# Ten staging tiles for layer 1's table, the plan read ahead of the fourth store, and a clear cut into four

## The reference, cut to what matters

```python
def _cgconv(x, src, dst, edge_attr, Wf, bf, Ws, bs, gamma, beta, rmean, rvar):
    z = jnp.concatenate([x[dst], x[src], edge_attr], axis=-1)      # 128 + 128 + 64
    msg = jax.nn.sigmoid(z @ Wf + bf) * jax.nn.softplus(z @ Ws + bs)
    summed = jax.ops.segment_sum(msg, dst, num_segments=n)
    cnt = jax.ops.segment_sum(jnp.ones((dst.shape[0],), x.dtype), dst, num_segments=n)
    out = summed / jnp.maximum(cnt, 1.0)[:, None]
    out = (out - rmean) * jax.lax.rsqrt(rvar + BN_EPS) * gamma + beta
    return out + x
...
x = _layernorm(x + cgconv(cgconv(x, layer 1), layer 2), axis=-1)
```

## Time and profile before

| | us |
|---|---|
| median of 3 runs | 2125.92 (2125.62 to 2128.58) |
| the profiled execution, its own time | 2123.97 |
| its span, first to last instruction | 2122.2 |

### The profile page before, as it was taken

The page is one execution under the profiler, slowest core; times in us unless marked ns, Lnnn a source line. Parts: engine busy times, 40 slices in busy tenths (PEclk is TensorE's granted clock), DMA queues, the critical chain, the costliest instruction groups (busy, mean ns, idle before and its releaser), DMA issues. The chain is left out here.

```text
span 2122.2 us, 35684 instructions
## 1 busy us (share of the span) xinstructions
PE 1561.2 (74%) x8321; PEld 1286.5 (61%) x8321; DVE 1801.6 (85%) x4351; ACT 1677.1 (79%) x2908; POOL 1513.2 (71%) x1589
## 2 busy tenths in 40 slices
PE   6877776777777777777487777777777777777773
PEld 5666665666566666666466666566665655666662
DVE  4799998989989889898648999899888887988887
ACT  3799887878878878787457888788878887887884
POOL 5577777777777777777257777777777777777770
PEclk8999999989999999999799999899999998998995
DMA  8355555555555555555375555555555555555542
GB/s 277 114 161 166 156 166 155 165 154 156 166 155 155 164 154 155 155 165 154 129 235 154 162 163 158 155 163 165 154 154 156 165 154 154 160 158 155 155 142 62
DMA packets 161806, 336.71 MB, mean 159 GB/s; under 512 B 58866, under 2 KB 85610, under 8 KB 161671
## 3 DMA queue, kind: packets, MB, share of 16 engines
q0 software_dynamic: 74496, 202.13, 32.1%
q1 hardware_dynamic: 85654, 131.58, 20.0%
q10 hardware_dynamic: 1522, 1.72, 0.3%
HBM read 315.49 MB, written 19.81 MB: 158 GB/s over the span
## 5 line engine op out<-in xcount | busy, mean ns | idle before, releaser
L343 POOL DMA_INDIRECT pre<-s_rows,ends x1512 | 1449.7, 959 | 488.7 <-issue 446.0
L457 PE MATMUL pre_ps<-rhs,lhs 128*128 128x256 f32 x3136 | 856.3, 418 | 462.7 <-DVE lhs L696 461.2
L457 PEld LDWEIGHTS pre_ps<-rhs,lhs 128*128 128x128 f32 x3136 | 608.4, 204 | 677.5 <-DVE lhs L696 390.0
L716 DVE TENSOR_TENSOR pre<-pre_ps,pre 128x1024 f32<-128x1024 f32 x378 | 460.4, 1218 | 50.7 <-DMA pre<-s_rows,ends 50.0
L546 ACT ACTIVATE pre<-pre 128x512 f32<-128x512 f32 x392 | 246.9, 630 | 307.7 <-DVE pre L716 268.9
L470 PEld LDWEIGHTS sum_ps<-hot,msg 128*128 128x128 f32 x3136 | 438.7, 203 | 51.8 <-issue 14.4
L696 DVE TENSOR_SCALAR lhs<-lhs,base_f,part 64x256 f32<-64x256 int32 x784 | 342.1, 436 | 114.8 <-issue 107.3
L470 PE MATMUL sum_ps<-hot,msg 128*128 128x64 f32 x3136 | 415.9, 278 | 23.8 <-DVE sums L736 23.8
L551 ACT ACTIVATE logs<-pre 128x1024 f32<-128x1024 f32 x392 | 414.4, 1057 | 12.4
L541 ACT COPY rhs<-dst_ps 64x256 f32<-64x256 f32 x792 | 290.0, 366 | 28.9 <-PE dst_ps L444 12.1
L727 DVE TENSOR_TENSOR msg<-soft_ps,logs 128x512 f32<-128x512 f32 x392 | 270.8, 691 | 13.6
(11 more groups left out here) (88 smaller groups left out, 570.1 us busy)
## 6 DMA issues: line engine op xcount, KB each, us to landing
lhs<-dge_and_destination_cols SPq DMA_DIRECT2D x196, 512.0 KB
pre<-s_rows,ends POOLq DMA_INDIRECT x1512
s_rows<-logs SPq DMA_DIRECT2D x10, 512.0 KB, 8.1
s_rows<-msg SPq DMA_DIRECT2D x7, 512.0 KB, 7.1
x_rows<-pre SPq DMA_DIRECT2D x12, 256.0 KB, 4.5
out<-y_out SPq DMA_DIRECT2D x12, 256.0 KB, 2.3
s_rows<-x_t SPq DMA_DIRECT2D x4, 512.0 KB, 11.9
ends<-edge_ends SPq DMA_DIRECT2D x100, 16.0 KB
```

Of the source, the lines that this page charges most:

```text
L343: nc.gpsimd.indirect_dma_start(pre[:, slot(k, j), i, 0:width], None, rows, bass.IndirectOffsetOnAxis(ap=ends[:, k, j * TILES + i, 0:1], ax ...
L457: ins = nc.tensor.matmul(pre_ps[:, j % 2, i, :], lhs[:, j // 2, edges], rhs[:, j, i // 2, :], start=True, stop=not plain(b, k, j))
L716: nc.vector.tensor_tensor(rows, pre_ps[:, j % 2], rows, ALU.add).then_inc(s_pre[j], 1)
```

## The change

Layer 1's table gets ten staging tiles in place of seven: the first three are in the part of `x1_t` that the sorted-destination test used (so ACT waits for `flagged` before it copies), then `logs`, `hot` and `msg`, then two more parts of `x1_t`. Only stores 10, 11 and 12 use a tile again (0, 1 and 2). `read_plan` now stands behind store 2. ACT's writes to `x1_t` begin three steps later (steps 3 to 27), and wait for the last stores out of tiles 0 to 2 and, at step 15, for tiles 8 and 9. DVE's clear of the counts is cut into four pieces of 1,600 columns, one at the end of each of steps 0 to 3, ahead of `one_hot`; step 4 waits for them.

```diff
         if first:
-            s_stage = [t["x1_t"][:, r * 4 * F2:(r + 1) * 4 * F2].rearrange("p (w f) -> p w f", f=F2) for r in (3, 4)] + s_stage
+            in_x1 = [t["x1_t"][:, r * 4 * F2:(r + 1) * 4 * F2].rearrange("p (w f) -> p w f", f=F2) for r in range(5)]
+            s_stage = in_x1[0:3] + s_stage[0:2] + s_stage[4:5] + s_stage[2:4] + in_x1[3:5]
...
-        log_stages, msg_stages, hot_stage = ((2, 3), (4, 5), 6) if first else ((0, 1), (2, 3), 4)
+        log_stages, msg_stages, hot_stage = ((3, 4), (6, 7), 5) if first else ((0, 1), (2, 3), 4)
...
             if first:
-                for c in range(5):
+                for c in range(3):
                     store_s(c)
                 bodies, at = read_plan()
-                for c in range(5, STORES):
+                for c in range(3, STORES):
                     store_s(c)
...
             if first:
+                act.wait_ge(flagged, 1)
                 for i in range(DOUBLES):
                     stage_double(i)
...
-                    step = SLOTS * k + j
-                    if first and isinstance(b, int) and step == 12:
-                        for r in (0, 1):
+                    step = SLOTS * k + j - 3
+                    if first and isinstance(b, int) and step in (0, 12):
+                        for r in ((0, 1, 2) if step == 0 else (8, 9)):
                             act.wait_ge(s_out[r], stores_of(r))
-                    if first and isinstance(b, int) and step < DOUBLES:
+                    if first and isinstance(b, int) and 0 <= step < DOUBLES:
...
             if first:
-                nc.vector.memset(t["sums"][:, 1, :], 0.0).then_inc(zeroed, 1)
                 v.wait_ge(iotas, 3)
-                v.wait_ge(zeroed, 2)
...
+                if first and isinstance(b, int) and SLOTS * k + j == 4:
+                    v.wait_ge(zeroed, 5)
...
+                if first and isinstance(b, int) and step < 4:
+                    nc.vector.memset(t["sums"][:, 1, step * (NPAD // 4):(step + 1) * (NPAD // 4)], 0.0).then_inc(zeroed, 1)
```

## The result

| | before | changed |
|---|---|---|
| median of 6 runs each | 2125.77 us (2123.27 to 2128.58) | 2115.65 us (2112.61 to 2118.41) |
| the profiled execution | 2123.97 us | 2112.61 us |
| its span | 2122.2 us | 2110.8 us |
| mean granted clock | 0.924 | 0.925 |

The ratio is 0.9954, with a 95% interval of 0.9942 to 0.9965: 10.1 us sooner by the medians. The forecast was 2116.3, in a range of 2112.5 to 2121.5. The changed kernel's profiled execution is the fastest of its six, so between the two traces there are 11.4 us to account for and not 10.

The account below looks back on a forecast made before the run. POOL's gather stream was taken as the bound, so only an earlier start counts: 8.6 + 0.5 + 1.6 - 1.1 = 9.6 us off the 2125.92 us median gives 2116.3 us, range 2112.5 to 2121.5.

Parts of the forecast that it names:

- The bound and the carry: POOL's gather stream, continuous from step 12, sets the pace; time saved ahead of step 5's softplus shortens the whole run equally.
- Part 1: Table's end: with ten stages ACT's last copy waits for PE, not a store, ending at 32.3 for 40.9; gain 8.6 us.
- Part 2: SP's queue: `read_plan` behind store 2 sends base loads near 21.4, and later stores still land in time; gain or loss zero.
- Part 3: Last table copy to step 2's turned rows: the same 15.9 us as before, so step 2 at 48.2.
- the first rival: Start of the steps: clock stays at 2.4 GHz through step 0, saving about 2.2 us; 2114.6 us, chance 0.12.
- Part 4: ACT's `x1_t` writes three steps later: 0.5 us less PE wait for `rhs`, and 1.6 us because the clock holds.
- Part 5: DVE's clear in four pieces, steps 0 to 3: three hidden, the fourth delays step 4; loss 1.1 us.
- The sum: Step 5's softplus 9.6 us sooner, carried by POOL to the end: median 2116.3 us.

Follow-up runs that it names:

- The held PE: The changed kernel with PE made to wait, behind the table, for the store out of a `msg` stage: 2130.21 us, ratio 1.0011.
- the late plan: The changed kernel with `read_plan` back behind the fifth store, the pieces of the clear kept: 2117.25 us, ratio 0.9958.
- the clear in two: The changed kernel with three quarters of the clear ahead of the steps and the last quarter in step 0: 2117.81 us, ratio 0.9957.
- The later writes alone: The kernel before, with only ACT's writes to `x1_t` moved three steps later: 2123.58 us, ratio 0.9987.
- clear on POOL: The changed kernel with POOL clearing the counts in one instruction after its last `x_rows` gather, none on DVE: 2120.48 us, ratio 0.9981.
- the stages alone: The changed kernel with `read_plan` back behind the fifth store and the clear one instruction ahead of the steps: 2113.49 us, ratio 0.9946.

## Why the prediction was right, point by point

**The bound and the carry: right.** POOL's stream ran on from step 12 without a wait, and step 12's 10.95 us are in the span as 11.4 (0.45 more, within the spread of such stretches). The held PE turned this into a test: 12.27 us at step 12, and a ratio of 1.0011.

**Part 1, 8.6 us: right, with 9.3 measured** (40.9 to 31.57). PE finished the table half a microsecond sooner, at 30.95 instead of 31.41; that end isn't the change's doing and lies between 30.35 and 32.56 in the eight traces, so the term is good to about 1 us. The wait for `flagged` was taken as free, and is, though not without a trace: ACT's first table load stood ahead of that wait and now stands behind it, and the first copy begins at 10.23 us instead of 9.03:

```profile
8.93 1.28 ACT L516 ACT_TABLE_LOAD   x1 [8.93 <-PE pre_ps L395]
```

By 11.68 ACT was back at PE's heels, and nothing of it is seen at the table's end.

**Part 2, zero: right.** The base loads went out at 20.65 (forecast 21.4), `hot` was late by 0.81 us (forecast under 1), and the late plan costs 0.5 us at step 0. The hole in the DMA engines' work was expected at 26 to 29; the stretches of the changed kernel show shares of 0.48 (24 to 26 us) and 0.56 (26 to 28), against 0.23 in the earlier trace rows, so it is shallower. One reader of the stores was timed wrongly: POOL's step 7 was to wait for the softplus, at 52, and waits for the last store, to 49.58.

**Part 3, step 2 at 15.9 us behind the last copy: wrong.** It is 13.62, and 2.3 us are gained that I had counted at zero: the step that failed is taking the same length over from layer 2. Layer 2's row was chosen, where the clock stood at 0.53. The start of layer 2 is code that the change doesn't touch, and it doesn't always go that way. PE's timelines there, in the kernel before, then in the changed one, then with the clear in two, the first matmuls of step 0:

```profile
1085.27 0.67 PE L442 MATMUL dst_ps<-w_node,x_cols 128*128 128x256 f32 x2 [1.64 <-ACT msg L515]
1087.37 1.19 PE L442 MATMUL dst_ps<-w_node,x_cols 128*128 128x256 f32 x2 [1.32 <-ACT rhs L541]
```

```profile
1075.55 0.67 PE L443 MATMUL dst_ps<-w_node,x_cols 128*128 128x256 f32 x2 [1.25 <-issue]
1077.65 0.67 PE L443 MATMUL dst_ps<-w_node,x_cols 128*128 128x256 f32 x2 [1.32 <-ACT rhs L543]
```

```profile
1076.20 0.67 PE L443 MATMUL dst_ps<-w_node,x_cols 128*128 128x256 f32 x2 [1.26 <-ACT msg L516]
1078.30 1.19 PE L443 MATMUL dst_ps<-w_node,x_cols 128*128 128x256 f32 x2 [1.32 <-ACT rhs L543]
```

In the first the clock fell behind idle times of 1.64 and 1.32 us (1.19 us for the second pair). In the second it held behind 1.25 and 1.32, and step 1 came 5.16 us behind step 0 instead of 6.45. In the third it fell behind 1.26 and 1.32. So the idle times of PE just ahead don't decide it. I had taken one row as what such a start always does, and it was one of two outcomes. In layer 1 PE now comes from the table after 0.72 us, and there the clock held in each of the five traces in which PE came from the table after 0.72 to 0.94 us. The two parts of the 2.3 us are 1.27 up to step 0 (4.73 to 3.46) and 1.05 to step 1 (6.21 to 5.16). The held PE lost the first part again and not the second, since its clock came back sooner: what a start at the lower level costs depends on when it ends. What came in steps 0 and 1 is the first rival, the quicker first step, to which I gave 0.12; it forecast 2.2 us less 0.5 for `hot`, and 2.3 came. The rule cited there, that activity releases the throttle, agrees with layer 1's rows, and the outcome drawn from it was the better guess than that one row.

**Part 4, 0.5 + 1.6 us: right.** PE's wait for `rhs` is 1.55 us (forecast 1.46), the clock is at 1.00 from 48 to 50, and steps 2 to 3 take 6.39 us instead of 8.30: 1.9. The later writes alone show the whole 2.1. In all six traces in which that wait was 1.55 us the clock held; it fell with the waits of 1.95 (before) and 3.59 us (clear on POOL). Two readings of rows were off and changed nothing: the clock fell not during the wait but at its end (it is still 0.95 of full from 58 to 59 us), and the matmuls of 1.06 us at 58.77, taken as the length at the lower level, lie across that fall; wholly at that level they are 1.19 us long.

**Part 5, 1.1 us lost: right, with 1.1.** Steps 3 to 4 take 6.38 instead of 5.45, 0.93; the piece of step 2 costs 0.17 more, which is counted in part 4's 1.9 above. The pieces are 1.39 us long, not 1.35, with 0.28 ahead of each. The place was right: only where DVE had waited 0.27 us for PE does a piece show in full.

**What the prediction didn't have.** The clock was followed through step 3 only. In the changed kernel waits of 2.79 us (to 59.6) and 1.68 (to 67) stand in PE's row, the clock falls near 69, and step 6 comes 1.7 us late. What makes it fall stays open. In steps 3 to 6 it fell not at all with the stages alone, once in the kernel before, in the changed kernel, with the plan late, with the clear in two and with the later writes, twice with PE held and three times with the clear on POOL. The clear in two and the stages alone have the same waits of PE there, and only one fell. Each fall in steps 5 and 6 cost 1.7 us, the one at step 3 before 1.6.

**The sum** at step 12: 9.3 + 2.3 + 1.9 - 0.9 - 1.7 = 10.9, and 10.95 measured. The forecast of 9.6 is near it since two errors of about 2 us, the quicker steps 0 and 1 and the later fall of the clock, cancel. That closeness is luck; what isn't is the largest term, part 1.

**What each edit is worth.** The stages, with the later writes, bring all of it. The later writes brought some 2 us at step 3 and the stages the rest, by the rows; ten stages without the later writes weren't run. The early plan brings 0.5 us at step 0, the pieces lose about 1.1 at step 4, and neither can be seen in a time: 0.9946, 0.9954, 0.9957 and 0.9958 have intervals that overlap. No version tried beats the changed kernel beyond doubt; the stages with the later writes would be the simpler one to keep.

## What to carry to other kernels

Ask which buffer the last operation of a start-up phase waits for, and which transfer must leave it: here the store stood behind `read_plan` in SP's queue and was issued only at 27.67, and three more stages took the wait away without moving the plan. Work that lay hidden in such a wait (here the clear) stays hidden as long as another engine's work still covers it, so move it only if the trace shows it bare. Don't take the clock of one trace as what a place in the code always gets: the same code with the same waits ran at either level here. A start of several steps can hold one fall or none, so put a range of one or two falls, 1.7 us each here, on such a forecast.

## What the hardware showed that I had not expected

- A clear of 128 x 6400 on POOL stopped DVE's copies for its whole 5.45 us (0.30 to 5.60 us), above. An idle engine isn't a free one.
- It may go the other way round too. Some of POOL's gathers issued beside a piece of the clear on DVE take longer. The first gather of step 7, shown above, lay beside the piece at 48.95; the next such row lay beside the piece at 55.34:

```profile
55.48 2.34 POOL L344 DMA_INDIRECT pre<-s_rows,ends  x1 [0.30 <-issue]
58.12 0.95 POOL L344 DMA_INDIRECT pre<-s_rows,ends  x1 [0.30 <-issue]
```

  1.85 and 2.34 us where their neighbours take 0.94 or 0.95, and without pieces the same gather took 0.94 (at 49.91, the stages alone). The second is longer by the 1.39 us of a piece. Such rows stand in each kernel with pieces there, but the overlap wasn't tested by itself, and it can't be the whole cause: a gather from `x_rows` at 36.79 in the changed kernel lay beside the first piece (36.33 to 37.72) and took 0.94.
- On two of the chips every version of this kernel that was run took a third longer, with instructions of the same length on all engines but PE, and engines that wait for something that the trace doesn't hold.
